# Cross attention on one core: a PSUM bank for each head's context, the softmax weights back in one transfer, and the second head's scores behind the whole first key product

## What is computed

```
def _cross_attention(q_in, kv_in, wq, bq, wk, bk, wv, bv, wo, bo, bias_k, bias_v):
    qh = (q_in @ wq + bq).reshape(b, q_len, H, K)
    kh = (kv_in @ wk + bk).reshape(b, t, H, K)
    vh = (kv_in @ wv + bv).reshape(b, t, H, K)
    kh = jnp.concatenate([kh, broadcast(bias_k)], axis=1)      # one extra key, one extra value
    vh = jnp.concatenate([vh, broadcast(bias_v)], axis=1)
    weights = softmax(einsum('bqhk,bthk->bhqt', qh, kh) / sqrt(K))
    ctx = einsum('bhqt,bthk->bqhk', weights, vh).reshape(b, q_len, H * K)
    return ctx @ wo + bo
x = x + attention_1(norm(x), ctx);  x = x + attention_2(norm(x), ctx);  x = x + mlp(norm(x))
```

## Time and profile before

| | us |
|---|---|
| median of 3 runs (3027.85 to 3033.89) | 3030.14 |
| the profiled execution, its own time | 3028.64 |
| its span in the profile | 3026.8 |
| PE busy | 2836.7 |
| DVE busy | 1860.2 |
| ACT busy | 1092.0 |

### The profile page before, as it was taken

How to read it: one execution, slowest core, us unless ns; L and a number is a source line. 1 busy time by engine, 2 the same in 40 slices (tenths; PEclk the granted TensorE clock), 3 DMA queues, 4 the chain that set the end, 5 groups by cost and what they waited for, 6 DMA issues and landing times.

```text
span 3026.8 us, 40813 instructions
## 1 busy us (share of the span) xinstructions
PE 2836.7 (94%) x14352; PEld 2122.0 (70%) x14352; DVE 1860.2 (61%) x2743; ACT 1092.0 (36%) x2409; POOL 535.2 (18%) x373
## 2 busy tenths in 40 slices
PE   5989898997989999999999999999999999999799
PEld 2333333334778888888888878788888888888687
DVE  5989989897765444465444574564444654444644
ACT  3232323223434334343333343343343443433332
POOL 2857667572010000000000010010000000000100
PEclk8999899998999999999999999999999999999899
DMA  5010010111242222222222211132222222222111
GB/s 161 1 29 28 18 39 2 55 42 42 83 164 91 76 97 80 79 83 75 97 80 74 92 60 63 56 103 75 97 80 88 79 70 97 80 88 71 46 52 56
DMA packets 146370, 215.69 MB, mean 71 GB/s; under 512 B 16176, under 2 KB 82736, under 8 KB 145168
## 3 DMA queue, kind: packets, MB, share of 16 engines
q1 hardware_dynamic: 143408, 210.73, 20.9%
q0 software_dynamic: 2880, 3.94, 0.6%
HBM read 164.53 MB, written 46.14 MB: 70 GB/s over the span
## 4 chain that ended last, share of the span: by engine, by line
PE 61%; DVE 4%; ACT 2%; issue 1%; DMA 1%; SPq 0%; ACTq 0%; DVEq 0%
PE ca_ps L60 18%; PE ca_ps L62 17%; PE ca_ps L61 17%; PE ca_ps L1991 4%; PE ca_ps L1982 4%; DVE ca_ct_lo L1749 1%; ACT ca_ct_hi L1559 1%; DVE ca_stats L68 1%; DMA xres<-pb_dram 1%; DMA pb_dram<-ca_pb 1%; PE ca_ps L2018 1%; SPq L1446 0%; DVE ca_pb L1745 0%; DVE ca_pr L1741 0%; ACT ca_pr L1552 0%
## 5 line engine op out<-in xcount | busy, mean ns | idle before, releaser
L1552 ACT ACTIVATE ca_pr<-ca_ps,ca_nb 128x129 f32<-128x129 f32 x512 | 181.0, 369 | 426.4 <-DVE ca_nb L1735 426.4
L60 PE MATMUL ca_ps<-ca_h_hi,ca_wq_hi 128*128 128x512 f32 x768 | 308.3, 401 | 4.2 <-DVE ca_h_lo L1780 3.7
L1505 POOL TENSOR_TENSOR ca_dv<-ca_bvr 128x256 f32<-128x256 f32 x32 | 23.6, 738 | 1601.5 <-DVE xq L1720 1442.0
L617 DVE TENSOR_TENSOR_SCAN tm_xn<-tm_wd,tm_vb 128x512 f32<-128x512 f32 x256 | 298.5, 1208 | 12.7
L62 PE MATMUL ca_ps<-ca_h_hi,ca_wq_lo 128*128 128x512 f32 x768 | 302.4, 394 | 0.0
L61 PE MATMUL ca_ps<-ca_h_lo,ca_wq_hi 128*128 128x512 f32 x768 | 301.3, 392 | 0.0
L60 PE MATMUL ca_ps<-ca_wv_hi,ca_ctx_hi 128*128 128x256 f32 x1024 | 296.3, 289 | 1.3 <-DVE ca_wv_lo L1715 1.3
L61 PE MATMUL ca_ps<-ca_wv_lo,ca_ctx_hi 128*128 128x256 f32 x1024 | 286.0, 279 | 0.0
L62 PE MATMUL ca_ps<-ca_wv_hi,ca_ctx_lo 128*128 128x256 f32 x1024 | 286.0, 279 | 0.0
L1749 DVE SCALAR_TENSOR_TENSOR ca_ct_lo<-ca_ps,ca_hv,ca_ct_hi 128x512 fp32r<-128x512 f32 x128 | 96.1, 751 | 278.1 <-ACT ca_ct_hi L1559 277.8
L60 PE MATMUL ca_ps<-ca_wo_hi,ca_ct_hi 128*128 128x512 f32 x640 | 255.3, 399 | 0.2 <-DVE raw L1755 0.2
(11 more groups left out here) (232 smaller groups left out, 5926.1 us busy)
## 6 DMA issues: line engine op xcount, KB each, us to landing
pb_dram<-ca_pb SPq DMA_DIRECT2D x128, 256.0 KB, 2.0
xres<-pb_dram SPq DMA_DIRECT2D x512, 64.0 KB, 1.9
ca_sq<-in_wq SPq DMA_DIRECT2D x49, 512.0 KB, 5.4
ca_so<-in_wo SPq DMA_DIRECT2D x48, 512.0 KB, 3.7
ca_sk<-in_wk SPq DMA_DIRECT2D x33, 512.0 KB, 6.5
ca_sv<-in_wv SPq DMA_DIRECT2D x32, 512.0 KB, 4.0
x_dram<-xres SPq DMA_DIRECT2D x8, 1024.0 KB, 4.2
ca_bvr<-in_bvb SPq DMA_DIRECT2D x32, 256.0 KB, 4.2
```

The source lines that it names most:

```text
L60: pe.matmul(out, lhs[0], rhs[0], start=first, stop=False)
L617: v.tensor_tensor_scan(state[t % 2][:, d, :], wd[:, g].rearrange("p b t -> p (b t)"), pair[:, d, :], 0.0, ALU.mult, ALU.add).then_inc(scan ...
L1552: ins = act.activation(pr[hd][:, b, :], ps[:, BANK_SC + b // 2, o:o + KW], ACT.Exp, bias=nbs[hd][:, b:b + 1], scale=SCALE, accum_out=sms[h ...
```

## The change

1. **Banks.** Head 0's context stays in bank 7, head 1's goes to bank 4. A context now waits only for the low part of the same head of the unit before.
2. **Weights.** The block transpose reads its source with a step of four elements (key = 4s + j in place of 32j + s), so that the way back from DRAM is one pattern of 128 partitions: one transfer of 256 KB in place of four of 64 KB.
3. **Scores.** In `slot` the scores of head 1 stand behind all four chunks of the key product.
4. **Passes.** In `passing` and `mlp_turn` both value products come ahead of both contexts. In the last `mlp_turn` the layer norm's transposes come ahead of the contexts. DVE's and ACT's orders follow.

```diff
-    BANK_Q, BANK_K, BANK_O, BANK_SC, BANK_PV = 0, 1, 2, 5, 7
+    BANK_Q, BANK_K, BANK_O, BANK_SC = 0, 1, 2, 5
+    CTX_BANKS = (7, 4)
...
-                sp.wait_ge(pt_in[hd], A.n * 64)
+                sp.wait_ge(pt_in[hd], A.n * 16)
...
-                for j in range(4):
-                    sp.dma_start(pT[hd][TB * j:TB * j + TB, :].rearrange("r (i x) -> r i x", i=4),
-                                 pb_dram[hd].rearrange("(i r) (j x) -> j r i x", i=4, j=4)[j]).then_inc(pt_in[hd], 16)
+                sp.dma_start(pT[hd].rearrange("p (i x) -> p i x", i=4),
+                             pb_dram[hd].rearrange("(i r) (j x) -> (r j) i x", i=4, j=4)).then_inc(pt_in[hd], 16)
...
-                v.transpose(pb[hd][:].rearrange("p j b s -> p b j s"), pr[hd][:, :, 0:L].rearrange("p b (j s) -> p b j s", s=TB)).then_inc(blocks_ready, 1)
+                v.transpose(pb[hd][:].rearrange("p j b s -> p b j s"), pr[hd][:, :, 0:L].rearrange("p b (s j) -> p b j s", s=TB)).then_inc(blocks_ready, 1)
...
             def second(A, C):
...
-                context_lo(A, 0)
                 split_one(wk, sk, wk_hi, wk_split, C.wkv + 1)
                 value_out(C, 1)
+                context_lo(A, 0)
                 context_lo(A, 1)
...
             def context(A, hd):
-                pe.wait_ge(pt_in[hd], A.n * 64 + 64)
+                pe.wait_ge(pt_in[hd], A.n * 16 + 16)
                 pe.wait_ge(v_out, A.n * 2 + 2)
-                pe.wait_ge(ct_split, A.n * 2 + hd)
+                if not (isinstance(A.g, int) and A.n == 0):
+                    pe.wait_ge(ct_split, A.n * 2 + (hd - 1))
...
             def passing(A, C):
...
                 value(C, 0, A.o * 4 - 1 if C.n > 1 else 0)
+                value(C, 1, A.o * 4 if C.n > 1 else 0)
                 context(A, 0)
-                value(C, 1, A.o * 4 if C.n > 1 else 0)
                 context(A, 1)
...
             def slot(A, C):
                 scores(A, 0)
                 query(C, 0, BANK_Q)
-                key(C, 0, (0, 1))
+                key(C, 0)
                 scores(A, 1)
-                key(C, 0, (2, 3))
                 query(C, 1, BANK_Q)
...
             def mlp_turn(A, C, M):
...
+                    value(C, 1, A.o * 4)
+                    context(A, 0)
+                    context(A, 1)
+                    pe.wait_ge(exp_done, A.n * 2 + 2)
+                    norm_transpose(M.ln, A.n * 2 + 2, A.n * 2 + 4)
+                else:
+                    pe.wait_ge(exp_done, A.n * 2 + 2)
+                    norm_transpose(M.ln, A.n * 2 + 2, A.n * 2 + 2)
+                    context(A, 0)
+                    context(A, 1)
```

More of the change, by code:

```diff
@@ L1558, in context_hi @@
                 wait_apart(act)
-                act.activation(cT[hd][0][:], ps[:, BANK_PV, :], ACT.Identity, bias=head_col(A, "bias_v", hd)).then_inc(ct_hi, 1)
+                act.activation(cT[hd][0][:], ps[:, CTX_BANKS[hd], :], ACT.Identity, bias=head_col(A, "bias_v", hd)).then_inc(ct_hi, 1)
             def roots(ln):
@@ L1605, in second @@
                 roots(C.ln)
+                split_one(wk, sk, wk_in, wk_hi, C.wkv + 1)
                 context_hi(A, 0)
-                split_one(wk, sk, wk_in, wk_hi, C.wkv + 1)
                 context_hi(A, 1)
@@ L1744, in normalise @@
                 v.wait_ge(blocks_out[hd], A.n * 16)
-                v.transpose(pb[hd][:].rearrange("p j b s -> p b j s"), pr[hd][:, :, 0:L].rearrange("p b (j s) -> p b j s", s=TB)).then_inc(blocks_ready, 1)
+                v.transpose(pb[hd][:].rearrange("p j b s -> p b j s"), pr[hd][:, :, 0:L].rearrange("p b (s j) -> p b j s", s=TB)).then_inc(blocks_ready, 1)
             def context_lo(A, hd):
                 v.wait_ge(ct_hi, A.n * 2 + (hd + 1))
-                v.scalar_tensor_tensor(out=cT[hd][1][:], in0=ps[:, BANK_PV, :], scalar=head_col(A, "bias_v", hd),
+                v.scalar_tensor_tensor(out=cT[hd][1][:], in0=ps[:, CTX_BANKS[hd], :], scalar=head_col(A, "bias_v", hd),
                                        in1=cT[hd][0][:], op0=ALU.add, op1=ALU.subtract).then_inc(ct_split, 1)
@@ L1865, in turn @@
                 value_out(C, 0)
+                value_out(C, 1)
                 context_lo(A, 0)
-                value_out(C, 1)
                 context_lo(A, 1)
@@ L1891, in mlp_turn @@
                     value_out(C, 0)
+                    value_out(C, 1)
                 context_lo(A, 0)
-                if C is not None:
-                    value_out(C, 1)
                 context_lo(A, 1)
@@ L1986, in context @@
             def context(A, hd):
-                pe.wait_ge(pt_in[hd], A.n * 64 + 64)
+                pe.wait_ge(pt_in[hd], A.n * 16 + 16)
                 pe.wait_ge(v_out, A.n * 2 + 2)
-                pe.wait_ge(ct_split, A.n * 2 + hd)
+                if not (isinstance(A.g, int) and A.n == 0):
+                    pe.wait_ge(ct_split, A.n * 2 + (hd - 1))
                 for b in range(4):
-                    ins = pe.matmul(ps[:, BANK_PV, b * L:(b + 1) * L], vT[A.quad][:, b, hd * P:(hd + 1) * P],
+                    ins = pe.matmul(ps[:, CTX_BANKS[hd], b * L:(b + 1) * L], vT[A.quad][:, b, hd * P:(hd + 1) * P],
                                     pT[hd].rearrange("p (i b s) -> p b i s", i=4, b=4)[:, b], start=True, stop=True)
@@ L2095, in mlp_turn @@
                     value(C, 0, A.o * 4 - 1)
-                context(A, 0)
-                if C is not None:
                     value(C, 1, A.o * 4)
-                context(A, 1)
-                pe.wait_ge(exp_done, A.n * 2 + 2)
-                norm_transpose(M.ln, A.n * 2 + 2, A.n * 2 + (2 if C is None else 4))
+                    context(A, 0)
[7 more added lines that the diff above has]
+                    context(A, 1)
                 attended(A, A.n * 2 + (2 if C is None else 4))
```

## The result

| | before, us | after, us |
|---|---|---|
| median (4 runs each) | 3029.34 (3027.85 to 3033.89) | 2986.31 (2985.30 to 2987.92) |
| ratio, 95% interval | | 0.9856 (0.9839 to 0.9873) |
| span of the profiled execution | 3026.8 | 2983.5 |
| granted clock, mean | 0.978 | 0.978 |

The change makes the kernel 43 us faster. The forecast was 2980 us with a range of 2970 to 2999: sign and range held, and the gain is 7 us smaller than forecast. The spans differ by 43.3 us, and that is the number that the rest divides up.

The account below looks back on a forecast made before the run. PE, busy for 94% of the span, was taken as the bound, so only its waits could be won. 43 - 3.5 + 8 + 3 = 50.5 us off 3028.6 gave 2978, forecast as 2980 us for the median, range 2970 to 2999.

Parts of the forecast that it names:

- The banks: Slots: a context no longer waits for the low part of the other head's context; 0.77 us each, 43 us.
- who is late next: Slots: the output product's k = 1 step slips, waiting for head 1's low part, by 0.03 or 0.10 us; -3.5 us.
- The scores: Slots: head 1's scores move later, its softmax is late by 0.15 us, cost zero.
- the weights in the slots: Slots: the one transfer takes 2.2 us to PE, head 1's weights are 2.1 us early, worth nothing.
- The last `mlp_turn`: Last `mlp_turn`: head 1's context starts 1.2 us earlier and the transposes no longer delay the output product; 3 us.
- The seven passes: Passes: the one transfer lets head 1's context start 1.17 us earlier in each of seven passes; 8 us.
- the transpose pays for its step: Rival: DVE's stepped block transpose takes up to twice 0.712 us, passes lose their gain; 2990 us, chance 0.12.
- no wait moved into the output product: Rival: the slots' wait moves into the output product, head 1's low part 0.3 us later; 2997 us, chance 0.12.
- the one transfer never landed late in a slot: Rival: the one transfer takes 6.5 us beside 512 KB loads, PE stalls in slots and passes; about 3130 us, chance 0.03.

Follow-up runs that it names:

- e1: The kernel before with nothing but the two banks and the context's new wait: 2992.67 us, ratio 0.9886.
- e4: The changed kernel with head 1's scores back between the halves of the key product: 2985.52 us, ratio 0.9864.
- e5: The kernel before with nothing but the stepped transpose and the one transfer: 3027.94 us, ratio 0.9998.
- e6: The changed kernel with the old orders in the passes and the last `mlp_turn`: 2987.31 us, ratio 0.9855.
- e7: The kernel before with each transpose cut in halves, head 1's read with a step of two elements, head 0's contiguous: 3034.05 us in one execution.
- e3b: The changed kernel with DVE's transpose contiguous and ACT reading the key product from PSUM with a step of four elements: 2984.90 us, ratio 0.9859.
- e9: e3b with DVE's layer norm statistics cut up in the passes and the output weights' split behind head 1's transpose: 2975.10 us, ratio 0.9826.
- e10: The changed kernel, stepped transpose kept, with DVE's layer norm statistics cut up and the output weights' split moved in the passes: 2982.28 us, ratio 0.9841.
- e3: The changed kernel with DVE's transpose contiguous and ACT writing the keys to SBUF with a step of 32 elements: 2983.44 us, ratio 0.9848.

## Why the prediction was right, and where it was wrong

**The banks and who is late next: right.** Forecast 43 - 3.5 = 39.5 us in the slots, measured 39.9, and e1 shows that the bank makes it. The slip too is where and as large as forecast. In a slot in which DVE splits the key weights, the low part of head 1 ends at 1520.40 (1519.66 + 0.74), and the k = 1 matmul that needs it runs late: its row is longer and the next one starts 0.33 behind it in place of 0.23. In the slots between, both are as usual.

```profile
1520.47 0.49 PE L60 MATMUL ca_ps<-ca_wo_hi,ca_ct_hi 128*128 128x512 f32 x1
1520.80 0.39 PE L61 MATMUL ca_ps<-ca_wo_lo,ca_ct_hi 128*128 128x512 f32 x1
```

**The scores and the weights in the slots: right at zero** (e4, e5), but with half the spare that I had worked out. The stepped transposes and the slower transfer make head 1's weights later; in the 56 slots after they land 1.1 us (median) before their context starts, 0.4 at the least, where the forecast was 2.1.

**The last `mlp_turn`: right in size, and partly by luck.** Forecast 3, measured 2.9 (e6: 3.0). From the scores of head 1 to the output product it is 14.71 us (2773.72 to 2788.43), and it was 17.84 (2814.00 to the 2831.84 of the earlier trace rows). Two things in this sum aren't as forecast. The store of head 1's weights took 3.44 us in the profile before, some 1.4 more than usual, and PE waited for it; in e7, with the order of before and a store of 2.08, the same stretch takes 16.84, so that of the 3.1 us one is the late store's. And I had 1.2 us from weights that come earlier. After, the contexts wait for no weights at all: PE waits 7.03 us for the layer norm (L1768) and then runs transposes and contexts without a gap. So the transposes fill time in which PE had waited for the weights, and 0.82 us of waiting for a low part (the row of 2788.43) is all that comes back.

**The seven passes: wrong, 8 us forecast, 0.5 measured.** Two terms were mis-sized. The first: the step of the prediction was 3.37 us from the issue of the weights to context 1, less 2.2 for the one transfer. Here are SP and PE in the same pass after (the earlier trace rows before):

```profile
1346.76 0.33 SPq L1442 DMA_DIRECT2D pb_dram<-ca_pb  x1
1348.79 0.38 SPq L1446 DMA_DIRECT2D xres<-pb_dram  x1
1351.15 0.32 SPq L1442 DMA_DIRECT2D pb_dram<-ca_pb  x1
1353.17 0.37 SPq L1446 DMA_DIRECT2D xres<-pb_dram  x1
```

```profile
1353.29 1.05 PE L1991 MATMUL ca_ps<-xres,xq 128*128 128x128 f32 x8
1356.00 1.16 PE L1991 MATMUL ca_ps<-xres,xq 128*128 128x128 f32 x8 [1.65 <-DMA xres<-pb_dram]
```

From issue to context it is 1356.00 - 1353.17 = 2.83 us: the transfer takes 2.7, not the 2.0 of the store of the same size, and a pass wins 0.54 in place of 1.17. The estimate for 256 KB from the Trainium skill ("DMA: Bandwidth & Descriptors", on the anatomy of one DMA), 2.6 us, was the nearer one, though that section's figures are for transfers that GpSimd issues and these are SP's; I had set it aside for the store's row.

The second is a rival that I had given 0.12: the transpose pays for its step. Its sign stood in the prediction (L1745 over 1 us), and it came. DVE in the same pass, the row maximum of head 0 and SP's issue of head 1's store before:

```profile
1352.84 0.70 DVE L1733 TENSOR_REDUCE ca_mx<-ca_ps 128x4 f32<-128x516 f32 x1 [4.85 <-PE ca_ps L1982]
...
1362.11 0.34 SPq L1441 DMA_DIRECT2D pb_dram<-ca_pb  x1
```

and DVE after:

```profile
1341.13 0.69 DVE L1733 TENSOR_REDUCE ca_mx<-ca_ps 128x4 f32<-128x516 f32 x1 [4.96 <-PE ca_ps L1981]
...
1345.63 1.09 DVE L1745 STREAM_TRANSPOSE ca_pb<-ca_pr 128x512 f32<-128x512 f32 x1
1346.66 0.65 DVE L1733 TENSOR_REDUCE ca_mx<-ca_ps 128x4 f32<-128x516 f32 x1
...
1350.03 1.09 DVE L1745 STREAM_TRANSPOSE ca_pb<-ca_pr 128x512 f32<-128x512 f32 x1
```

Both transposes lie in one chain on DVE, from head 0's row maximum (1341.13) to head 1's store (1351.15). It takes 10.02 us and took 9.27. The same chain in six of the seven passes (all but the first), medians, with the transfer behind it:

| us | before | after | e3b | e9 | e10 |
|---|---|---|---|---|---|
| row maximum of head 0 to store of head 1 | 9.27 | 10.02 | 9.26 | 8.43 | 9.20 |
| transfer's issue to ACT's high part of head 1 | 4.6 | 4.1 | 4.1 | 4.1 | 4.1 |

The chain is 0.75 longer by twice 0.39, and 0.5 shorter behind it: a pass loses 0.2 us or so in place of winning 1.2. The start-to-start rows show it too: from head 1's high part in h0's `turn` to the one in the `second` behind it, it is 29.63 us before, 29.89 after and 29.13 in e3b. With the step off (e3b) the chain is back at 9.26, and with the statistics cut up it is 0.8 shorter, with either transpose. So the mechanism of e10 is right, though its stretches don't show it in full. The `mlp_turn` of h0 is the exception among the six: 12.85 before and 12.24 after, because in the profile before the clock had fallen there and DVE waited 1.28 us for the scores of head 1, behind the transpose.

The rule of the Trainium skill that the prediction names ("SBUF — State Buffer", note on 16-byte cachelines) says that a read with fewer than two hits a line pays. Two f32 a line (e7) are free and one (L1745 at 1.10 us) is not: the traces agree with it. They don't agree with what the same note makes of it, that one can stride for free by 4 fp32, which is the step of L1745. I had the rule before me and gave its case 0.12, for want of a row. The 2990 us of that rival was too dark, since it took the transpose to double (it grew 1.55 times) and only 1 us to be left at the end.

**The rest, by one profile.** By the mechanism alone seven passes would be 7 x 0.25 = 1.7 us slower than before. PE's waits for the weights there say much the same: 7.9 us before (the 17.7 of the earlier trace rows less 9.3 in the last pass and 0.6 in a slot), 9.3 after. By the stretches they are 0.5 faster. Of this difference of 2.2, 1.1 lies ahead of the cross attention, and 1.4 is the clock that fell in the `mlp_turn` of h0 before and not after; against it stands a fall of 1.6 that only the changed kernel has, below. What then is left, some 1.3, isn't explained; it is of the size of what comes and goes between executions.

The other rivals: no wait moved into the output product (12.7 us of hidden loads against 11.2), and the one transfer never landed late in a slot. That rival took the 6.5 us of the earlier trace rows for the most that a 512 KB load takes; it is the median. The total came within the range because the banks, the large term, were right; the passes' miss is about the whole of what the forecast was off by.

## What to carry to other kernels

A wait that recurs in every slot with the same size is worth its PE gap from start to start, not its idle time, times the number of slots: here a free PSUM bank gave 40 of 43 us. A rearrangement of the data that saves DMA issues has to be priced on the engine that then reads or writes with a step, and where that engine's chain ends a stretch it can cost more than the transfers did; here the step was free in ACT's read of PSUM (16 bytes), and in DVE's read of SBUF at 8 bytes. Once the steady slots are full, look at what stands on DVE between a softmax and its store in the passes: moving it gave 0.8 us a pass, more than the whole transfer part of this change.

## What the runs showed of the hardware

**Steps.** DVE's block transpose of 128x512 f32 from SBUF takes 0.71 us with no step and 1.10 with a step of 16 bytes; halves take 0.85 together with no step and with a step of 8 bytes alike. ACT's write of 128x512 f32 to SBUF with a step of 128 bytes takes 1.19 us against 0.69; its read from PSUM with a step of 16 bytes 0.69 as without.

**Late stores.** A store of 256 KB to DRAM is mostly followed by its transfer back after 2.0 to 2.1 us. In every profile a few of 128 take longer: in the passes 3.09 and 3.44 before, 2.49, 2.70 and 2.49 after, 3.89 in e10, up to 4.63 in e3. No slot of the changed kernel waits for it; in a pass PE mostly does (2.36 us behind the 2.70 after, 2.92 behind e3's 4.63).

**The clock.** The `mlp_turn` of h0 has PE idle for 3.2 us in all executions (before: 3.18, after: 3.19). In 7 of the 12 profiled ones (before among them) the granted clock then fell to 1.2 GHz for some 3 us in the key product that follows, and in the others it did not. Rows of stretches: length, busy times of PE, PEld, DVE, ACT and POOL, granted clock, DMA share and GB/s; first e10, then before.

```profile
1731.00:1735.00 4.00, 0.82 (x7) 0.62 (x7) 3.76 (x5) 1.51 (x8) 0.00 (x0) 1.00 0.00 0
...
1736.00:1739.00 3.00, 3.00 (x9) 2.35 (x8) 1.84 (x3) 0.00 (x0) 0.00 (x0) 0.50 0.08 31
```

```profile
1758.00:1762.00 4.00, 3.90 (x12) 3.12 (x13) 3.89 (x13) 0.00 (x0) 0.00 (x0) 0.67 0.00 0
```

Seven matmuls then follow each other at 0.43 us in place of 0.23, which costs 1.4 us. After a late store it can happen in a `second` too. In the changed kernel head 1's context waited 2.36 us for weights whose store had taken 2.70, and the transposes behind it ran at the low clock:

```profile
2389.00:2393.00 4.00, 1.64 (x15) 1.45 (x14) 3.63 (x4) 0.69 (x1) 3.98 (x3) 1.00 0.55 197
2393.00:2396.00 3.00, 3.00 (x19) 3.00 (x18) 0.75 (x1) 0.69 (x1) 2.63 (x3) 0.57 0.00 0
```

The unit after this pass took 33.66 us; in e6, e9, e1 and e4, where the clock stayed up there, it took 31.99 to 32.01. The changed kernel's 88.12 against e6's 86.02 in the table is this and the late store. In e10 the same place cost 1.9 by a store of 3.89 and 1.6 by the clock, and the `mlp_turn` of h0 another 1.4: without these 4.9 us its stretches would be 7.6 us shorter than the changed kernel's in place of 2.7. But the changed kernel's own 2.3 must then come off too, which leaves 5, short of the 6 to 9 expected and near 7 x 0.8. What decides whether the clock falls after the same idle time, and why some stores are late, stays open. A change to a pass that is worth 1 us can't be read from the stretches of one profile, while the chain's length repeats to 0.03 us in five of the six passes, before and after.
